# Value products of two key tiles issued as one piece, in a transformer and mixture-of-experts kernel on one NeuronCore

## The chip, the core and the metric

The kernel runs on one core of one Trainium2 chip. A core has five engines, each working through its own list of instructions in order: TensorE (PE in the profile; its weight loads are shown apart as PEld), VectorE (DVE), ScalarE (ACT), GpSimd (POOL) and SyncE (SP, which here only starts DMAs). They meet at semaphores. TensorE reads SBUF and writes PSUM, the accumulation memory, which the other engines empty.

The metric is the device time of one execution in microseconds (us), the median of several. Lower is better.

## The reference

The program is a six-layer transformer with self-attention, cross-attention and a feed-forward part, followed by one mixture-of-experts layer, over 4 batches of 512 tokens of width 256. The part that the change touches is the attention, 16 heads of width 16, run twice in each layer:

```
def _attn(q, k, v, mask):
    scores = jnp.einsum('bqhd,bkhd->bhqk', q, k) / np.float32(np.sqrt(HD))
    scores = jnp.where(mask[:, None, None, :], jnp.float32(-jnp.inf), scores)
    w = jax.nn.softmax(scores, axis=-1)
    return jnp.einsum('bhqk,bkhd->bqhd', w, v)
...
for i in range(NL):
    xn = _adaln(x, noise_emb, n1_w[i], n1_b[i])
    ... q, k, v, _rope ...
    a = _attn(q, k, v, src_mask).reshape(B, L, D) @ so_w[i].T
    x = x + a
    ... the same with the context's keys and values (cross-attention) ...
    xn = _adaln(x, noise_emb, n3_w[i], n3_b[i])
    h = jax.nn.gelu(xn @ f1_w[i].T + f1_b[i], approximate=False)
    x = x + (h @ f2_w[i].T + f2_b[i])
```

## The kernel before

**Jobs and slots.** A job is one attention of one batch: 8 in a layer (4 self, 4 cross), 48 in all. The work on a job is spread over three consecutive stretches of the program, called slots. In slot k the kernel makes the maxima of the scores of job k (pass 1), the exponentials and value products of job k-1 (pass 2), finishes job k-2 (division by the sums, output projection), and prepares queries and keys of job k+1. Slots whose finished job is a cross-attention also run the feed-forward part of that batch; they use the table of places `LONG`, the others `SHORT`. 25 short and 22 long slots have both pass 1 and pass 2 in them. The loop `Fori` runs over layers.

**Units.** A slot has 16 units (`SLOT_UNITS`). A unit is one key tile of 128 of one group of four heads: unit u is tile u % 4 of group u // 4. TensorE's order inside a unit is written out by hand: score product 0 of pass 2 (line 832), two pairs of score products of pass 1 (line 859), score product 1 of pass 2, side work of place 2u, score product 2, the value product of the previous unit (line 845), score product 3, side work of place 2u+1. Places thus run from 0 to 31, two for each unit; the tables `SHORT` and `LONG` say at which place each piece of side work stands.

**Hand-over of pass 2.** A score product of pass 2 writes one of two PSUM banks (`RING2 = 2`), ScalarE takes its exponential into `prob` (line 908), and product n may start when exponential n-2 is done. `prob` has 8 places, two units. The value product of a unit is four products of 32 columns each, which stand beside each other in the array and accumulate in `psv`; after the four tiles of a group ScalarE copies `psv` to `osum` (line 916), SP writes it to DRAM (line 525), and each of the four groups has a place of its own in `osum`.

**Hand-over of pass 1.** Two pairs of banks. VectorE takes the maximum of each pair (line 1070); pair n may start when maximum n-2 is done.

**Side work.** All of it goes through one PSUM bank, `side`, so a piece may start only when the piece before it has been read. The names: `HT` and `LT` transpose normalised rows (line 732; ScalarE reads), `HQ` and `HK` project queries and keys (line 738; VectorE reads, lines 1096 and 1097), `HV` projects values (line 746; ScalarE reads), `O` is the output projection (line 746; VectorE reads), `F1` and `F2` are the feed-forward products (lines 807 and 818; VectorE reads, lines 1106 and 1113), `M` moves the maxima. `SPLIT` are the places at which ScalarE makes the high and middle parts of queries and keys, `RECIP` and `NORM` those at which VectorE takes the reciprocal of the sums and multiplies (lines 1166 and 1170), `LN_HT` and `LN_LT` those of the normalisations, `GELU` that of the activation.

**The finish of a job.** The last group's copy stands in unit 0 of the next slot. Then SP writes it, POOL waits for the write (`pool_fence`, line 677), loads the sums (`den`), waits for the reciprocal, writes `inverse`, loads it again broadcast (shown as `nT`, line 695), VectorE multiplies at `NORM`, and TensorE does `O`. SP's order in a slot: last group's write of job k-2, context and weights where needed, first group's write of job k-1, the parts of job k+1 and the loads of its first half of heads (`load_first`, `load_second`, 12 transfers with their mask rows, lines 551, 553 and 562), the second and third group's writes, and then the loads of the second half of heads, which wait until pass 2 of the slot is over.

## Time and profile before

| | us |
|---|---|
| median of 3 runs | 4339.0 (4333.73 to 4340.74) |
| the profiled execution, device time | 4337.09 |
| its span, first to last instruction | 4335.3 |
| a short slot | 63.1 |
| long slots | 94.0 to 102.3 |
| after the last exponential (last finishes, experts) | 349.2 |

In the rows, `PE L832 MATMUL ps<-qstack,kstack ... x2` is a group of two products of source line 832. A row of a timeline gives the start in us, the time from the first start to the last end in the group, engine, line, operation, output and inputs, the shapes, the count and, in brackets, how long the engine had been idle before and who ended that. A row of a table by stretch gives the stretch, its length, and the busy time and instructions of each engine. The modelled end of a product lies behind the start of the next, so starts are compared with starts below. An f32 product is two records, one for each of its two passes.

### The profile page before, as it was taken

The numbers are of one execution on the slowest core, as the hardware profiler recorded it, in microseconds if no ns is written. First come the engines' busy times: TensorE is split into PE (matmuls) and PEld (weight loads), VectorE is DVE, ScalarE is ACT, GpSimd is POOL, SyncE is SP. The second block draws the span as 40 slices with busy tenths as digits, with TensorE's granted clock in tenths as the row PEclk, the third lists the DMA queues.
The fourth block names the chain that finished last, engine by engine and source line by source line (L and its number), as shares of the span: only waits on it lengthen the run. The fifth ranks groups of instructions, "written<-read, shape, count | busy, mean of one in ns | idle before, by whom it ended". The sixth has DMA issues, their size and how long they took to land. (4 is left out here: it accounts for less than half of the span.)

```text
span 4335.3 us, 66534 instructions
## 1 busy us (share of the span) xinstructions
PE 3833.6 (88%) x19478; PEld 1695.2 (39%) x19478; DVE 2841.1 (66%) x4476; ACT 2498.6 (58%) x4206; POOL 1148.4 (26%) x1280
## 2 busy tenths in 40 slices
PE   3899899899899899899999899999999999897558
PEld 1233344433344433344433344433344433343446
DVE  6788766688666688766688766588766688751411
ACT  1577655577655567655567655567655577654112
POOL 3233222232222232322232322232322232301043
PEclk8999999999999999999999999999999999999779
DMA  5655534445533355433356443456443366521235
GB/s 160 157 153 145 131 80 94 107 137 145 131 81 91 97 145 141 132 90 82 93 150 148 125 95 82 94 145 153 123 99 80 91 171 154 132 54 46 68 103 112
DMA packets 334220, 500.30 MB, mean 115 GB/s; under 512 B 53705, under 2 KB 242257, under 8 KB 333521
## 3 DMA queue, kind: packets, MB, share of 16 engines
q1 hardware_dynamic: 289680, 430.95, 39.0%
q0 software_dynamic: 44160, 64.73, 6.3%
q8 instruction: 184, 3.01, 0.3%
q14 instruction: 196, 1.60, 0.1%
HBM read 278.54 MB, written 222.58 MB: 116 GB/s over the span
## 5 line engine op out<-in xcount | busy, mean ns | idle before, releaser
L908 ACT ACTIVATE prob<-ps 128x512 f32<-128x512 f32 x3072 | 1751.3, 595 | 1249.8 <-PE ps L832 1246.9
L1070 DVE TENSOR_REDUCE negmax<-ps 128x2 f32<-128x1024 f32 x1536 | 1814.8, 1217 | 362.4 <-PE ps L859 332.5
L832 PE MATMUL ps<-qstack,kstack 114*128 114x512 bf16 x3072 | 1144.6, 390 | 118.0 <-ACT prob L908 99.0
L845 PE MATMUL psv<-prob,v 128*32 128x512 f32 x6144 | 826.7, 610 | 0.0
L832 PEld LDWEIGHTS ps<-qstack,kstack 114*128 114x128 bf16 x3072 | 273.9, 97 | 1269.3 <-ACT prob L908 935.7
L859 PE MATMUL ps<-kstack,qstack 49*128 49x512 bf16 x3072 | 487.8, 387 | 78.7 <-DVE negmax L1070 53.3
L677 POOL TENSOR_TENSOR pool_fence<-eps 128x1 f32<-128x1 f32 x288 | 55.2, 192 | 1688.0 <-ACT mrow L975 1026.5
L807 PE MATMUL side<-nT,wf 128*128 128x256 f32 x1536 | 375.0, 387 | 31.9 <-ACT mrow L975 18.3
L1106 DVE TENSOR_SCALAR hT<-side,f1b 128x256 f32<-128x256 f32 x384 | 167.5, 478 | 295.6 <-PE side L807 295.5
L818 PE MATMUL side<-wf,hT 128*128 128x256 f32 x1536 | 350.1, 381 | 3.5 <-DVE x L1113 1.8
L807 PEld LDWEIGHTS side<-nT,wf 128*128 128x128 f32 x1536 | 285.4, 191 | 88.2 <-ACT mrow L975 22.3
L818 PEld LDWEIGHTS side<-wf,hT 128*128 128x128 f32 x1536 | 290.2, 190 | 46.9 <-issue 4.6
L648 POOL TENSOR_TENSOR rot<-ropep 128x512 f32<-128x512 f32 x94 | 118.9, 1265 | 631.5 <-DVE ropep L1097 627.2
L651 POOL TENSOR_TENSOR rot<-rot,parts 128x1024 f32<-128x1024 f32 x94 | 200.7, 2136 | 280.7 <-ACT parts L943 280.7
L657 POOL TENSOR_TENSOR low<-rot,parts 128x1024 bf16<-128x1024 f32 x94 | 200.2, 2130 | 234.7 <-ACT parts L947 234.7
L859 PEld LDWEIGHTS ps<-kstack,qstack 49*128 49x128 bf16 x3072 | 95.2, 94 | 424.7 <-issue 309.5
L1113 DVE TENSOR_TENSOR x<-x,side 128x256 f32<-128x256 f32 x96 | 40.4, 421 | 303.5 <-PE side L818 303.5
L845 PEld LDWEIGHTS psv<-prob,v 128*32 128x32 f32 x6144 | 121.5, 108 | 274.4 <-issue 223.8
L738 PE MATMUL side<-xnT,wself 128*128 128x512 f32 x384 | 195.2, 632 | 23.6 <-DVE ropep L1097 21.0
L746 PE MATMUL side<-wcross,hT 128*128 128x256 f32 x384 | 106.0, 425 | 53.7 <-DVE hT L1170 52.6
L732 PE MATMUL side<-ident,hT 128*128 128x128 f32 x592 | 97.2, 289 | 61.6 <-DVE ropep L1097 33.7
L943 ACT ACTIVATE parts<-rot 128x1024 bf16<-128x1024 f32 x96 | 100.7, 1049 | 63.1 <-POOL rot L649 44.3
(170 smaller groups left out, 3626.8 us busy)
## 6 DMA issues: line engine op xcount, KB each, us to landing
bounce<-parts SPq DMA_DIRECT2D x480, 256.0 KB, 2.5
qstack<-bounce SPq DMA_DIRECT2D x384, 192.0 KB, 6.1
kstack<-bounce SPq DMA_DIRECT2D x384, 192.0 KB, 6.6
value_sums<-osum SPq DMA_DIRECT2D x192, 256.0 KB, 6.5
bounce<-low SPq DMA_DIRECT2D x96, 256.0 KB, 2.1
hT<-value_sums POOLq DMA_DIRECT2D x96, 256.0 KB, 4.8
nT<-inverse POOLq DMA_DIRECT2D x96, 256.0 KB, 3.8
ctxT<-in_ctxT SPq DMA_DIRECT2D x24, 512.0 KB, 5.3
```

Of the source, the lines that this page charges most:

```text
L648: nc.gpsimd.tensor_tensor(rot[:, 0, :], ropep[:, 0, :], ropep[:, 1, :], ALU.subtract).then_inc(s_rot, 1)
L651: nc.gpsimd.tensor_tensor(rot[:, :, :], rot[:, :, :], parts[w][:, 0, :, :], ALU.subtract).then_inc(s_r1, 1)
L657: nc.gpsimd.tensor_tensor(low[:, :, :], rot[:, :, :], parts[w][:, 1, :, :], ALU.subtract).then_inc(s_low, 1)
L738: mm = nc.tensor.matmul(bank, w[:, k, m * P:(m + 1) * P], act_T[:, k, :], start=(k == 0), stop=(k == KD - 1))
L807: mm = nc.tensor.matmul(bank[:, i * D:(i + 1) * D], wf1[:, kk, f * P:(f + 1) * P], nT[:, kk, th * (S // 2):(th + 1) * (S // 2)], start=(kk ...
L818: mm = nc.tensor.matmul(bank[:, 0:D], hT[th][:, f, t * P:(t + 1) * P], wf2[:, f, :], start=(f == 0), stop=(f == FT - 1))
L832: nc.tensor.matmul(ps2[:, n % RING2, :], kk[0:ROWS, h, kt * P:(kt + 1) * P], q[0:ROWS, h, :], start=True, stop=True).then_inc(s_p2full, 1)
L845: mm = nc.tensor.matmul(psv[32 * i:32 * i + 32, 0, :], v[j % 2][:, kt, (HD + 1) * h:(HD + 1) * h + 32], prob[:, 4 * (u % 2) + i, :], start ...
L859: mm = nc.tensor.matmul(ps1[:, 2 * (n % 2) + e, :], qs[j % 2][rows, 8 * e + m, t * P:(t + 1) * P], ks[j % 2][rows, 8 * e + m, :], start=Tr ...
L908: nc.scalar.activation(prob[:, 4 * (u % 2) + i, :], ps2[:, n % RING2, :], ACT.Exp, scale=HD ** -0.5).then_inc(s_prob, 1)
L1070: nc.vector.tensor_reduce(out_at, ps1[:, 2 * (n % 2):2 * (n % 2) + 2, :], AX, ALU.max, negate=True).then_inc(s_p1free, 1)
L1106: ins = nc.vector.tensor_scalar(hT[th][:, f, :], bank[:, i * D:(i + 1) * D], f1b[:, f:f + 1], None, ALU.add)
```

## The change

The order of TensorE within a unit now depends on whether u is even or odd. Value products of two units are issued as one piece, in every second unit, before score product 2 of the even unit. `prob` has ten places, for which a function gives the place of each exponential, and ScalarE takes its exponentials three and one in odd units. `osum` has two places in place of four, so a copy of groups 2 and 3 first waits for the write of groups 0 and 1, with a semaphore for each. SP issues the loads of the second half of heads at the start of the slot in which they are used, behind the last group's write, no longer at the end of the slot before. And the tables of places are new.

```diff
 SHORT = {
-    "M": [25, 0], "HV": [1, 3], "HT": [6, 8], "HQ": [9, 11], "HK": [12, 14], "O": [18, 20],
-    "SPLIT": (14, 16, 19, 21), "PARTS": 23, "RECIP": 8, "NORM": (14, 15),
+    "M": [25, 0], "HV": [1, 2], "HT": [5, 6], "HQ": [9, 10], "HK": [13, 14], "O": [18, 21],
+    "SPLIT": (13, 15, 18, 21), "PARTS": 23, "RECIP": 6, "NORM": (11, 12),
...
 LONG = {
-    "M": [27, 0], "HV": [1, 3], "HT": [6, 8], "O": [11, 12], "HQ": [14, 15], "HK": [16, 18], "LT": [17, 19],
-    "F1": [20, 21, 22, 23, 24, 25, 26, 27], "F2": [28, 29, 30, 31],
-    "SPLIT": (17, 19, 21, 23), "GELU": (24, 28), "PARTS": 25, "RECIP": 5, "NORM": (9, 10),
+    "M": [29, 0], "HV": [1, 2], "HT": [5, 6], "HQ": [9, 10], "O": [11, 13], "HK": [14, 15], "LT": [17, 18],
+    "F1": [19, 20, 21, 22, 23, 24, 25, 26], "F2": [27, 28, 30, 31],
+    "SPLIT": (13, 15, 19, 21), "GELU": (23, 27), "PARTS": 25, "RECIP": 5, "NORM": (8, 9),
...
-    "LN_LT": dict(stats=[12, 12, 12, 12], aggregate=13, guess=13, newton=14, tiles=[14, 14, 15, 15]),
+    "LN_LT": dict(stats=[13, 13, 13, 13], aggregate=14, guess=14, newton=15, tiles=[15, 15, 16, 16]),
...
-        prob = sb("prob", [P, 8, S])
+        prob = sb("prob", [P, 10, S])
-        osum = sb("osum", [P, 4, S])
+        osum = sb("osum", [P, 2, S])
...
+        def prob_at(u, i):
+            two = 2 * (u % 2) + i // 2
+            return 2 * (two - 1 if two else 3 + u // 2 % 2) + i % 2
...
 # SP, in slot()
                 if tail:
                     write_sums(k - 2, 3)
+                if k and p1:
+                    load_first(k, 1)
+                    load_second(k, 1)
...
-                if head:
-                    load_first(k + 1, 1)
-                    load_second(k + 1, 1)
...
 # PE
-            def pv(j, u):
+            def pv(j, pair):
+                if pair % 2 == 0 and (j > 0 or pair > 0):
+                    pe.wait_ge(s_os, place.jobs(j, 4) + pair // 2)
+                pe.wait_ge(s_prob, place.jobs(j, 64) + 8 * pair + 8)
+                for u in (2 * pair, 2 * pair + 1):
...
+                    if p2 and u % 2 == 1:
+                        pass2(k - 1, u, 2)
                     for what, c in plan[2 * u]:
                         side_work(k, what, c)
-                    if p2:
+                    if u and u % 2 == 0 and p2:
+                        pv(k - 1, u // 2 - 1)
+                    elif u == 0 and tail:
+                        pv(k - 2, SLOT_UNITS // 2 - 1)
+                    if p2 and u % 2 == 0:
                         pass2(k - 1, u, 2)
-                    if u and p2:
-                        pv(k - 1, u - 1)
-                    elif u == 0 and tail:
-                        pv(k - 2, SLOT_UNITS - 1)
...
 # ACT
             def copy_group(k, j, g):
-                if j > 0 and g == 0:
-                    wait_sums(act, place, j - 1)
-                act.wait_ge(s_pv, place.jobs(j, 16) + 4 * g + 4)
-                nc.scalar.activation(osum[:, g, :], psv[:, 0, :], ACT.Copy).then_inc(s_os, 1)
+                if g >= 2:
+                    act.wait_ge(s_sums[j % 2][g % 2], place.at(32 * (j // 2) + 16, 16 * NJ))
+                elif j > 0:
+                    act.wait_ge(s_sums[(j - 1) % 2][g % 2], place.at(32 * ((j - 1) // 2 + 1), 16 * NJ))
+                act.wait_ge(s_pv, place.jobs(j, 8) + 2 * g + 2)
+                nc.scalar.activation(osum[:, g % 2, :], psv[:, 0, :], ACT.Copy).then_inc(s_os, 1)
```

TensorE, a short slot from the maxima's piece of unit 12 on, before: `ps<-qstack,kstack` are score products of pass 2, `ps<-kstack,qstack` those of pass 1, `psv` the value product.

```order
L793 MATMUL side<-identb,mpart 16x128 x4
L832 MATMUL ps<-qstack,kstack 128x512
L859 MATMUL ps<-kstack,qstack 128x512 x4
L832 MATMUL ps<-qstack,kstack 128x512 x2
L845 MATMUL psv<-prob,v 32x512 x4
L832 MATMUL ps<-qstack,kstack 128x512 x2
L859 MATMUL ps<-kstack,qstack 128x512 x4
L832 MATMUL ps<-qstack,kstack 128x512 x2
L845 MATMUL psv<-prob,v 32x512 x4
```

And now, the same engine and stretch:

```order
L801 MATMUL side<-identb,mpart 16x128 x4
L840 MATMUL ps<-qstack,kstack 128x512
L867 MATMUL ps<-kstack,qstack 128x512 x4
L840 MATMUL ps<-qstack,kstack 128x512 x4
L867 MATMUL ps<-kstack,qstack 128x512 x4
L840 MATMUL ps<-qstack,kstack 128x512
L853 MATMUL psv<-prob,v 32x512 x8
L840 MATMUL ps<-qstack,kstack 128x512 x3
```

Between two pieces of value products there were four score products of pass 2; now there are eight, and four of them stand in a row between two groups of pass 1.

TensorE, units 7 and 8 of a long slot before, with the second query projection and the key projections:

```order
L738 MATMUL side<-xnT,wcross 128x512 x2
L832 MATMUL ps<-qstack,kstack 128x512
L859 MATMUL ps<-kstack,qstack 128x512 x4
L832 MATMUL ps<-qstack,kstack 128x512
L738 MATMUL side<-ctxT,wcross 128x512 x2
L832 MATMUL ps<-qstack,kstack 128x512
L845 MATMUL psv<-prob,v 32x512 x4
L832 MATMUL ps<-qstack,kstack 128x512
L732 MATMUL side<-ident,hT 128x128 x4
```

And now, units 6 and 7 of a long slot on the same engine, from the second output projection to the second key projection:

```order
L754 MATMUL side<-wcross,hT 128x256 x4
L840 MATMUL ps<-qstack,kstack 128x512
L867 MATMUL ps<-kstack,qstack 128x512 x4
L840 MATMUL ps<-qstack,kstack 128x512 x2
L746 MATMUL side<-ctxT,wcross 128x512 x2
L840 MATMUL ps<-qstack,kstack 128x512
L746 MATMUL side<-ctxT,wcross 128x512 x2
```

Two pieces of side work of one odd unit had a score product, the value product and another score product between them; now a single score product stands there.

SP, from the end of one slot into the next, before:

```order
L562 DMA qstack<-bounce 48x2048
L562 DMA kstack<-bounce 48x2048
L626 DMA expert_rows<-in_empty 16x10400
L525 DMA value_sums<-osum 128x512
L608 DMA ctxT<-in_ctxT 128x2x512
```

And now, the same engine and border:

```order
L532 DMA value_sums<-osum 128x512 x2
L634 DMA expert_rows<-in_empty 16x10400
L532 DMA value_sums<-osum 128x512
L558 DMA qstack<-bounce 48x2048
L558 DMA kstack<-bounce 48x2048
```

The write of the last group came behind the loads of the second half of heads; now these loads come behind it.

## Rows read from the trace of the kernel before

**Rows 1.** The page, busy time of each engine.

```profile
PE 3833.6 (88%) x19478; PEld 1695.2 (39%) x19478; DVE 2841.1 (66%) x4476; ACT 2498.6 (58%) x4206; POOL 1148.4 (26%) x1280
```

**Rows 2.** Stretches: a short slot; first and last first-long slot; another long slot.

```profile
1700.00:1763.13 63.13, 59.78 (x322) 19.70 (x320) 51.49 (x69) 44.82 (x80) 20.44 (x24) 1.00 0.57 146
456.37:557.24 100.87, 91.64 (x457) 44.78 (x456) 62.42 (x105) 57.12 (x91) 22.77 (x25) 0.97 0.43 112
3714.00:3813.30 99.30, 90.24 (x457) 44.14 (x454) 62.82 (x105) 56.91 (x92) 22.59 (x25) 0.98 0.41 107
1210.26:1306.26 96.00, 89.59 (x457) 44.24 (x456) 62.55 (x105) 56.68 (x90) 22.77 (x25) 1.00 0.37 90
```

**Rows 3.** Timeline, units 13 to 15 of a short slot, value products and what follows.

```profile
1756.13 0.64 PE L845 MATMUL psv<-prob,v 128*32 128x512 f32 x4
...
1756.59 0.61 PE L845 MATMUL psv<-prob,v 128*32 128x512 f32 x4
...
1757.13 0.60 PE L832 MATMUL ps<-qstack,kstack 114*128 114x512 bf16 x2
```

**Rows 4.** Timeline of the last unit of that slot, PE, ACT and DVE.

```profile
1760.01 0.61 PE L832 MATMUL ps<-qstack,kstack 114*128 114x512 bf16 x2
...
1760.44 1.08 ACT L908 ACTIVATE prob<-ps 128x512 f32<-128x512 f32 x2 [0.72 <-PE ps L832]
...
1760.55 0.60 PE L859 MATMUL ps<-kstack,qstack 49*128 49x512 bf16 x4
...
1760.93 1.18 ACT L908 ACTIVATE prob<-ps 128x512 f32<-128x512 f32 x2
...
1760.98 2.36 DVE L1070 TENSOR_REDUCE negmax<-ps 128x2 f32<-128x1024 f32 x2 [0.53 <-PE ps L859]
...
1761.09 0.39 PE L832 MATMUL ps<-qstack,kstack 114*128 114x512 bf16 x1
...
1761.58 0.39 PE L832 MATMUL ps<-qstack,kstack 114*128 114x512 bf16 x1
...
1761.90 1.07 PE L845 MATMUL psv<-prob,v 128*32 128x512 f32 x8
```

**Rows 5.** Timeline of a long slot, side work and its readers.

```profile
1342.57 0.68 DVE L1096 TENSOR_TENSOR ropep<-side,cos 128x512 f32<-128x512 f32 x1
...
1343.90 1.98 PE L738 MATMUL side<-xnT,wself 128*128 128x512 f32 x4 [0.22 <-DVE ropep L1097]
...
1352.39 0.66 PE L732 MATMUL side<-ident,hT 128*128 128x128 f32 x4 [1.60 <-DVE ropep L1097]
...
1361.32 0.38 PE L832 MATMUL ps<-qstack,kstack 114*128 114x512 bf16 x1
...
1361.52 0.88 DVE L1106 TENSOR_SCALAR hT<-side,f1b 128x256 f32<-128x256 f32 x2 [0.39 <-PE side L807]
```

**Rows 6.** Timeline of the first long slot of a layer (starts 456.37), finish of a job.

```profile
461.64 0.34 SPq L525 DMA_DIRECT2D value_sums<-osum  x1
...
470.19 0.19 POOL L677 TENSOR_TENSOR pool_fence<-eps 128x1 f32<-128x1 f32 x1 [9.66 <-DMA value_sums<-osum]
...
474.70 0.55 DVE L1166 RECIPROCAL recip<-den 128x64 f32<-128x64 f32 x1 [5.11 <-DMA den<-value_sums]
475.17 4.55 DVE L1070 TENSOR_REDUCE negmax<-ps 128x2 f32<-128x1024 f32 x4
...
476.39 0.60 PE L859 MATMUL ps<-kstack,qstack 49*128 49x512 bf16 x2 [3.59 <-DVE negmax L1070]
```

**Rows 7.** Timeline of another long slot (starts 1210.26), finish of a job.

```profile
1214.10 0.59 ACT L916 ACTIVATE osum<-psv 128x512 f32<-128x512 f32 x1
...
1231.84 0.69 DVE L1170 TENSOR_TENSOR hT<-hT,nT 128x512 f32<-128x512 f32 x1 [2.32 <-DMA nT<-inverse]
```

**Rows 8.** Waits of TensorE: us in total, times, longest.

```profile
PE side L746 <- DVE hT L1170: 52.6, 21, 15.8
```

**Rows 9.** The tile osum: from issue of its writes to landing.

```profile
DMA to landing us min/median/max: 2.0/6.5/9.4
```

More of the change, by code:

```diff
@@ L383, in layers @@
         s_os = sem("pv_group_copied")
-        s_sums = [sem(f"value_sums_written{i}") for i in range(2)]
+        s_sums = [[sem(f"value_sums_written{i}{h}") for h in range(2)] for i in range(2)]
         s_den = sem("probability_sums_loaded")
@@ L485, in wait_sums @@
         def wait_sums(eng, place, j):
-            eng.wait_ge(s_sums[j % 2], place.at(64 * (j // 2 + 1), 32 * NJ))
+            for h in range(2):
+                eng.wait_ge(s_sums[j % 2][h], place.at(32 * (j // 2 + 1), 16 * NJ))
+        def prob_at(u, i):
+            two = 2 * (u % 2) + i // 2
+            return 2 * (two - 1 if two else 3 + u // 2 % 2) + i % 2
         def norms(place, k, what, add=0):
@@ L964, in side_work @@
                     if k >= 2:
-                        act.wait_ge(s_pv, place.jobs(k - 1, 16))
+                        act.wait_ge(s_pv, place.jobs(k - 1, 8))
                     dst = v[k % 2][:, 2 * c:2 * c + 2, 0:H * (HD + 1)].rearrange("p t (h e) -> p t h e", h=H)[:, :, :, 0:HD]
```

30 lines of the change are left out of this document (15 added, 15 removed).

## The prediction

> **What bounds the kernel now.** First the page's busy times [rows 1]: TensorE is at work 88% of the span, VectorE 66%, ScalarE 58%. The question is what TensorE waits for, and that is read by slot. All short slots but those at a loop border take 63.1 us, the six long slots that come first in their layer 99.3 to 102.3, the 16 other long ones 94.0 to 99.1, 97.3 in the mean [rows 2]. Then one unit without side work, start by start [rows 4]. From the score product at 1760.01 to the one at 1762.90 a unit takes 2.88 us. Its steps: score product to the next 0.23; into and out of pass 1 0.31 each; the two pairs of pass 1 0.23 apart; score product to value product 0.31; value product to the next score product 1.00, from 1756.13 to 1757.13 [rows 3]. These add to 2.61 us; the missing 0.27 is product 2 waiting for exponential 0. So a short slot is TensorE's work, 57.6 us (16 times 2.61, and 15.8 of side work by its starts), and 5.5 us of such waits. A long one is 85.7 us of work (43.9 of it side work) and 8 to 16 us of waits.
>
> The hand-overs have fixed lengths, which I use below. Score product to its exponential 0.43 (1760.01 to 1760.44); exponentials 0.49 apart (1.08 less the 0.59 of one); exponential to the score product two later 0.65 (1760.93 to 1761.58); pass-1 pair to its maximum 0.43 (1760.55 to 1760.98); maxima 1.14 apart (2.36 less 1.22) [rows 4]; maximum to the pair two later 1.22 (475.17 to 476.39) [rows 6].
>
> **What the joint piece saves.** One pass of a value product to the next takes 0.46 us, the last pass to the score product 0.54 (1756.13, 1756.59, 1757.13) [rows 3]. Leaving costs 0.09 more than staying. Entering costs 0.31 where score product to score product costs 0.23, again 0.09. A joint piece has four passes, three of 0.46 and one of 0.54: 1.91 us. Each pair of units saves 0.18, a slot 1.45, the 48 jobs 69 us. That is all that TensorE's work loses.
>
> **What it costs in short slots.** The score products keep two banks. I follow a pair of units without side work from score product 2 of the even unit, t = 0, just behind the joint piece. Product 3 is at 0.23; exponentials 2 and 3 start at 0.43 and 0.92. Odd product 0 must wait until 0.43 + 0.65 = 1.08, exponential 0 is at 1.51. Pass 1 is at 1.39 and 1.61, product 1 at 1.92, its exponential at 2.35. Product 2 at 2.15, exponential at 2.84; product 3 at 2.35 + 0.65 = 3.00; even product 0 at 2.84 + 0.65 = 3.49. The next pass 1 would be at 3.80 and 4.02, but the second maximum of the odd unit starts at 1.39 + 0.43 + 1.14 = 2.96, so it is at 4.18. Then product 1 at 4.49, the joint piece at 4.80, and product 2 again at 6.70. Two such units take 5.76 now. So a pair without side work **loses 0.94 us**: during the 1.91 us of the joint piece ScalarE has two banks of work and VectorE two pairs, and after it eight score products run at the pace of ScalarE and of the two banks. Side work in both halves of a pair fills exactly these holes: with 1.72 us in each, the same steps give 8.50, of which 8.49 is work.
>
> A short slot by pairs of units, from the same steps with its side work and ScalarE's extra pieces in their new places, us before and after: units 0 and 1 9.47, 9.26; 2 and 3 6.57, 7.40 (ScalarE's readings of the two transposes delay the exponentials); 4 and 5 9.21, 9.06; 6 and 7 9.23, 9.06; 8 and 9 7.98, 7.79; 10 and 11 8.18, 7.9; 12 and 13 6.70, 7.13; 14 and 15 5.76, 6.70. Sum 63.1 before, 64.3 after: **1.2 us slower**, 25 slots, 30 us. The waits go from 5.5 to 8.2.
>
> **What it costs in long slots.** Work is 84.2. Waits that go: in units 8, 12 and 13 TensorE now waits 1.60 us for VectorE's queue before the transpose [rows 5] and about 2 us around the activation. Waits that come:
> - Side work in both halves of an odd unit. The second piece needs the bank read, and only one score product (0.23) lies between; before, the value product lay there too. Reading a query or key piece takes 0.25 us to start, 1.29 for two multiplications (1342.57 to 1343.90 with release) and so 1.4 us of wait; a feed-forward piece 0.3 (end at 1361.22, 0.10 before the row at 1361.32, reader at 1361.52), 0.88 and release, 1.0 us of wait [rows 5]. There are six such units: 5, 7, 9, 11, 13, 15, with 1.4, 1.4, 1.1, 1.0, 1.0 and 0.5: 6.4 us.
> - In units 5 and 7 VectorE also comes late, since two maxima (2.3 us) stand ahead of the reading, in unit 11 and 13 a little: 3.6 us.
> - VectorE stands still at the first NORM, place 8, and with it the maximum behind it. It gets there about 18.7 us into the slot. The attention rows arrive about 21.5: the last copy starts at 4.9 (3.84 before [rows 7], but the joint piece is 0.9 longer), and the chain from copy to NORM took 17.7 (1214.10 to 1231.84) [rows 7], of which the write's landing loses about 1. VectorE then loses 2.8, of which TensorE sees about 1.
> - The pair with the two transposes 1.5, as in short slots; units 8 and 9 1.5 for the second normalisation; the rest 1.1.
>
> Sum 15.1, the slot 99.3 us. For the 16 ordinary ones that is +2.0 each, 32 us.
>
> **The moved loads.** In the first long slot of a layer the sums' write is issued at 461.64, behind 12 loads, and POOL goes on only at 470.19, 8.5 us later; VectorE waits 5.11 at the reciprocal, place 5, and TensorE 3.59 for the maxima behind it [rows 6]. Behind the change nothing stands ahead of this write, and writes of osum have landed in as little as 2.0 us (median 6.5) [rows 9]. So the sums are there at about 12 us into the slot and this stop goes: 101.2 to 99.3 in six slots, 11 us. The loads themselves are hidden: issued from 5.7 to 10.8 us into the slot, needed at unit 8, past 30. What is queued behind them on SP, the context, the first group's write at unit 4 and the parts, is due later. The two places of osum cost nothing if group 1's write, issued some 4.5 us before a slot ends, lands within 9.4, the longest of all [rows 9], since the copy that needs its place starts 4.9 into the next slot.
>
> One rule speaks against this move. The Trainium skill (DMA: Bandwidth & Descriptors, Issuing engines are not separate DMA queues) says that transfers of all issuers interleave on the same 16 DMA engines. By it POOL's loads of sums and rows, which now run while SP's 12 loads are in flight, would each come later; that is rival B below.
>
> **The sum.** 30 + 32 - 11 = 51 us on the profiled execution's 4337.1: 4388. The median is 1.9 above that execution, so **4390**. Terms not in the trace: the gap between the two units inside a joint piece, bounded by 0.46 and by 0.64 (all drain paid), taken as 0.46 because the two passes of one unit also load new weights; and the contention on POOL's loads, bounded by 0 and by 3 us a long slot.
>
> **Rivals.**
> - **A, faster: O finds its rows ready.** TensorE waited 52.6 us for NORM before O [rows 8], besides the stop at the reciprocal. If the sums' write lands in 2 us and POOL's loads are not held up, the rows are there before VectorE gets to NORM, the point being 18.7 us into the slot; the hold-up of units 4 and 5 (3.4 us with what follows from it) goes, and long slots take 95.9. Price: short +30, 16 slots -22, six -32: 4315. For it: write and loads landed late while queued behind or beside the stack loads. Against it: copy later by 1.1, and two chained POOL steps.
> - **B, slower still: the moved loads hold up POOL's chain.** If rows arrive 3 us later than 21.5, TensorE loses these 3 us in each of 22 long slots: 4390 + 66 = 4456. For it: 12 loads now start 0.2 us behind the sums' write. Against it: they are over at about 17 us.
> - **C: the joint piece saves nothing**, since going from one unit's weights to the next's within it costs the same 0.18: 4390 + 69 = 4459. Rows 3 speak against it.
>
> **Chances.** My forecast 0.60, A 0.24, B 0.09, C 0.03, others 0.04. A run of this kernel can tell about 0.2%, 9 us. Faster by more than that 0.27, within 0.07, slower 0.66. The range reaches from 4290, below A, for its bound is uncertain by a microsecond per slot, to 4450, just short of B: 4290 to 4450.
>
> **What would show it.** In the profile after: short slots of 64 to 65 us, all alike; a joint piece of 1.91 us; pairs of units 14 and 15 of 6.7; in long slots TensorE waiting at the second side piece of odd units, and 98 to 101 us; no wait of 5 us at the reciprocal. Short slots at or under 63.1 would mean that a hand-over is shorter than read here; long slots under 97 that VectorE's readings come earlier than I place them.

## The result

The changed kernel takes 4702.81 us (median of 4 runs, 4699.73 to 4713.41), the kernel before 4339.87 beside it (4333.73 to 4342.37). The ratio is 1.0843, 95% interval 1.0822 to 1.0864: 363 us slower, where 51 was forecast. The profiled execution has a span of 4711.7 us.

First the page's busy times of the changed kernel, answering [rows 1]:

```profile
PE 3891.9 (83%) x19478; PEld 1806.6 (38%) x19478; DVE 2847.2 (60%) x4476; ACT 2479.0 (53%) x4206; POOL 1156.0 (25%) x1280
```

The work is the same, the engines wait longer. Then three stretches, answering [rows 2]: a short slot, a first-long one, another long one. Columns are length, busy times of PE, PEld, DVE, ACT and POOL, granted clock, DMA share and GB/s.

```profile
1847.09:1912.31 65.22, 58.98 (x321) 21.17 (x321) 50.18 (x69) 44.21 (x80) 20.89 (x24) 1.00 0.56 138
1195.10:1306.71 111.61, 92.76 (x455) 47.09 (x454) 63.31 (x105) 55.97 (x91) 22.70 (x25) 0.92 0.37 92
1306.71:1419.13 112.42, 92.82 (x458) 47.86 (x456) 64.83 (x105) 55.95 (x90) 22.70 (x25) 0.92 0.32 77
```

First-long slots grew by 11 us in the mean, the other long ones by 13, and their clock, between 0.97 and 1.00 before, is 0.92. The joint piece itself does what it should; timeline of units 14 and 15 of that short slot, answering [rows 3] and [rows 4]:

```profile
1905.68 0.39 PE L840 MATMUL ps<-qstack,kstack 114*128 114x512 bf16 x1 [0.21 <-ACT prob L922]
...
1906.86 1.92 PE L853 MATMUL psv<-prob,v 128*32 128x512 f32 x16
...
1908.72 0.60 PE L840 MATMUL ps<-qstack,kstack 114*128 114x512 bf16 x2
...
1909.88 0.39 PE L840 MATMUL ps<-qstack,kstack 114*128 114x512 bf16 x1 [0.56 <-ACT prob L922]
```

From 1906.86 to 1908.72 it takes 1.86 us (forecast 1.91), and the pair of units 6.63 (forecast 6.70, 5.76 before). This is one of the better slots: the median of that pair over the 20 short slots counted below is 7.0 us.

The finish of a job in the long slot that starts at 1306.71, answering [rows 6] and [rows 7]:

```profile
1311.51 0.60 ACT L932 ACTIVATE osum<-psv 128x512 f32<-128x512 f32 x1
...
1312.14 0.32 SPq L532 DMA_DIRECT2D value_sums<-osum  x1
1312.59 2.01 SPq L558 DMA_DIRECT2D qstack<-bounce  x1
...
1315.86 0.19 POOL L685 TENSOR_TENSOR pool_fence<-eps 128x1 f32<-128x1 f32 x1 [4.96 <-DMA value_sums<-osum]
...
1322.65 0.59 POOL L699 DMA_DIRECT2D inverse<-recip  x1 [0.28 <-issue]
1329.16 0.18 POOL L685 TENSOR_TENSOR pool_fence<-eps 128x1 f32<-128x1 f32 x1 [5.92 <-DMA inverse<-recip]
...
1334.40 0.69 DVE L1186 TENSOR_TENSOR hT<-hT,nT 128x512 f32<-128x512 f32 x1 [8.82 <-DMA nT<-inverse]
...
1336.28 0.61 PE L867 MATMUL ps<-kstack,qstack 49*128 49x512 bf16 x2 [6.28 <-DVE negmax L1086]
...
1337.65 2.81 PE L746 MATMUL side<-xnT,wself 128*128 128x512 f32 x4
```

The sums' write leaves at once, as hoped. But the write of `inverse` needs 6.5 us to be seen (1322.65 to 1329.16), NORM comes 27.7 us into the slot, VectorE stands 8.8 us, TensorE 6.3. Behind that the four products of 512 columns take 2.81 us; the same four just before the stop took 1.88: the clock is at its lower level, 1.2 GHz. The loads of the second half of heads, issued up to 1319.11, landed up to 1328.82, and `inverse` at 1328.99.

Median time from issue to landing, changed kernel and then the kernel before:

```profile
hT<-value_sums POOLq DMA_DIRECT2D x96, 256.0 KB, 9.2
...
den<-value_sums POOLq DMA_DIRECT2D x48, 32.0 KB, 5.3
inverse<-recip POOLq DMA_DIRECT2D x48, 32.0 KB, 5.5
```

Before, these three are 4.8, 2.1 and 2.4 us. Last, units 7 and 8 of the same slot, all engines:

```profile
1357.32 2.14 POOL L665 TENSOR_TENSOR low<-rot,parts 128x1024 bf16<-128x1024 f32 x1 [5.87 <-ACT parts L963]
...
1357.94 1.54 DVE L1069 SCALAR_TENSOR_TENSOR lnv<-y 128x4 f32<-128x4 f32 x1
...
1359.54 1.27 POOL L656 TENSOR_TENSOR rot<-ropep 128x512 f32<-128x512 f32 x1
...
1359.71 1.12 DVE L1071 SCALAR_TENSOR_TENSOR y<-lnv,y 128x4 f32<-128x4 f32 x1
...
1360.77 1.26 POOL L657 TENSOR_TENSOR rot<-ropep 128x512 f32<-128x512 f32 x1
1360.86 1.64 DVE L1076 TENSOR_SCALAR hT<-x,mv,y 128x256 f32<-128x256 f32 x2
...
1364.41 0.90 PE L740 MATMUL side<-ident,hT 128*128 128x128 f32 x3 [4.25 <-DVE hT L1076]
```

An operation of four columns takes 1.54 us and ends at 1359.48, when POOL's ends (1359.46). The next ends at 1360.83, POOL's at 1360.81. TensorE waits 4.25 us for the tiles behind them. And behind this stop the clock is low again, as two feed-forward pieces of the same eight products show, the first in unit 9, the other two units later:

```profile
1370.03 3.77 PE L815 MATMUL side<-nT,wf 128*128 128x256 f32 x8 [0.87 <-ACT nT L953]
...
1378.99 1.89 PE L815 MATMUL side<-nT,wf 128*128 128x256 f32 x8
```

The two stretches of this slot at the lower clock, behind NORM and behind the second normalisation (columns as above):

```profile
1332.70:1339.51 6.81, 3.23 (x7) 1.24 (x8) 5.11 (x7) 1.09 (x2) 0.00 (x0) 0.50 0.07 26
1363.42:1373.64 10.22, 8.36 (x25) 4.88 (x25) 4.35 (x6) 4.56 (x7) 2.12 (x1) 0.50 0.15 49
```

TensorE is at work for 11.6 us of them at half its speed, so the lower clock costs this slot some 5.8 us (an estimate from these two rows).

### The profile page after: what moved, and what is told of

Its sections match the earlier page's. It is cut to its first block and busy times, and to the rows that moved or that the text cites. A ratio compares the mean times of both kernels' runs of the same rounds, so it can differ in the third digit from the quotient of the medians.

```text
span 4711.7 us, 66396 instructions
## 1 busy us (share of the span) xinstructions
PE 3891.9 (83%) x19478; PEld 1806.6 (38%) x19478; DVE 2847.2 (60%) x4476; ACT 2479.0 (53%) x4206; POOL 1156.0 (25%) x1280
## 5 line engine op out<-in xcount | busy, mean ns | idle before, releaser
L922 ACT ACTIVATE prob<-ps 128x512 f32<-128x512 f32 x3072 | 1717.8, 595 | 1572.2 <-PE ps L840 1564.9
L840 PE MATMUL ps<-qstack,kstack 114*128 114x512 bf16 x3072 | 1105.0, 399 | 190.8 <-ACT prob L922 172.7
L853 PE MATMUL psv<-prob,v 128*32 128x512 f32 x6144 | 752.8, 606 | 0.0
L867 PE MATMUL ps<-kstack,qstack 49*128 49x512 bf16 x3072 | 508.5, 397 | 196.7 <-DVE negmax L1086 173.2
L815 PE MATMUL side<-nT,wf 128*128 128x256 f32 x1536 | 397.2, 404 | 47.8 <-DVE hT L1122 25.6
L853 PEld LDWEIGHTS psv<-prob,v 128*32 128x32 f32 x6144 | 171.1, 110 | 315.7 <-issue 301.5
L746 PE MATMUL side<-xnT,wself 128*128 128x512 f32 x384 | 228.9, 727 | 49.2 <-DVE ropep L1113 48.0
L1186 DVE TENSOR_TENSOR hT<-hT,nT 128x512 f32<-128x512 f32 x96 | 79.4, 829 | 239.5 <-DMA nT<-inverse 239.3
L740 PE MATMUL side<-ident,hT 128*128 128x128 f32 x592 | 112.0, 321 | 111.5 <-DVE hT L1076 109.4
L1133 DVE TENSOR_TENSOR x<-x,side 128x512 f32<-128x512 f32 x96 | 66.1, 688 | 182.9 <-PE side L754 182.9
```

The source lines that it names most:

```text
L746: mm = nc.tensor.matmul(bank, w[:, k, m * P:(m + 1) * P], act_T[:, k, :], start=(k == 0), stop=(k == KD - 1))
L815: mm = nc.tensor.matmul(bank[:, i * D:(i + 1) * D], wf1[:, kk, f * P:(f + 1) * P], nT[:, kk, th * (S // 2):(th + 1) * (S // 2)], start=(kk ...
L840: nc.tensor.matmul(ps2[:, n % RING2, :], kk[0:ROWS, h, kt * P:(kt + 1) * P], q[0:ROWS, h, :], start=True, stop=True).then_inc(s_p2full, 1)
L853: mm = nc.tensor.matmul(psv[32 * i:32 * i + 32, 0, :], v[j % 2][:, kt, (HD + 1) * h:(HD + 1) * h + 32], prob[:, prob_at(u, i), :], start=( ...
L867: mm = nc.tensor.matmul(ps1[:, 2 * (n % 2) + e, :], qs[j % 2][rows, 8 * e + m, t * P:(t + 1) * P], ks[j % 2][rows, 8 * e + m, :], start=Tr ...
L922: nc.scalar.activation(prob[:, prob_at(u, i), :], ps2[:, n % RING2, :], ACT.Exp, scale=HD ** -0.5).then_inc(s_prob, 1)
```

## The experiments

Mean length of the slots in each profiled execution, from first exponential to first exponential: 20 short slots ("short"), the 4 short ones at the loop's border, which follow long ones and in which the cross-attention's weights are loaded ("behind long"), the 6 first-long ones and the 16 other long ones; the very first slot is left out. Two of the 20, in the first and in the last layer, also load these weights. Before they took 63 us like the rest; in the changed kernel they take 73.2 and 72.2, and the other 18 take 65.7. "Median" is device time; the kernel before was at 4331 to 4337 beside these runs.

| kernel | median | short | behind long | first-long | long |
|---|---|---|---|---|---|
| before | 4339.9 | 63.1 | 69.8 | 101.1 | 97.3 |
| changed | 4702.8 | 66.4 | 72.6 | 112.3 | 110.7 |
| e1 changed, loads back | 4598.8 | 65.8 | 68.0 | 111.1 | 107.0 |
| e2 before, loads moved | 4406.7 | 63.1 | 64.5 | 103.2 | 102.1 |
| e3 joint piece, old tables, old loads | 4589.9 | 68.2 | 72.2 | 108.1 | 102.3 |
| e4 before, new tables | 4499.7 | 64.3 | 68.8 | 108.1 | 103.4 |
| e5 changed, old tables | 4690.8 | 68.6 | 68.7 | 111.2 | 109.0 |
| e6 before, loads late in long slots | 4299.7 | 63.1 | 64.4 | 100.5 | 96.3 |
| e7 changed, loads late | 4627.2 | 66.3 | 72.6 | 109.9 | 106.7 |
| e8 as e7, old long table | 4530.7 | 66.3 | 72.3 | 107.2 | 101.7 |
| e9 as e6, self weights late | 4281.9 | 63.1 | 64.5 | 95.9 | 96.7 |
| e10 as e9, reciprocal at 4 | 4244.5 | 63.1 | 64.5 | 94.8 | 95.0 |
| e11 as e6, half exponentials | 4231.6 | 60.8 | 62.2 | 100.2 | 95.9 |
| e12 as e8, half exponentials | 4447.1 | 64.2 | 69.8 | 106.3 | 99.8 |
| e13 as e6, half maxima | 4211.2 | 62.5 | 62.8 | 98.5 | 93.1 |
| e14 as e8, half maxima | 4442.1 | 65.2 | 70.9 | 104.5 | 99.6 |
| e15 as e7, half maxima | 4494.4 | 65.2 | 71.3 | 106.0 | 102.0 |
| e16 joint piece, best of all this | 4442.0 | 65.7 | 64.8 | 102.0 | 101.0 |
| e17 as e7, short POOL operations | 4516.3 | 66.1 | 72.0 | 105.4 | 102.8 |
| e18 as e6, short POOL operations | 4271.2 | 62.9 | 64.5 | 100.2 | 95.3 |

### One part at a time: e1 to e5

```diff
# e1, on the changed kernel (e2, on the kernel before: the reverse)
-                if k and p1:
-                    load_first(k, 1)
-                    load_second(k, 1)
...
+                if head:
+                    load_first(k + 1, 1)
+                    load_second(k + 1, 1)
```

> The changed kernel with one part undone: the loads of the second half of heads are issued at the end of the slot before, as in the kernel before; joint piece, places of prob and osum, and tables stay new. Theory 1 (the moved loads hold up the chain of the finish: sums written, fence, sums loaded, inverse written and loaded, NORM at 27.7 us into the slot where I had 21.5; VectorE stands there, TensorE behind it): long slots go from 109-113 to 99-102 us, NORM is at 19 to 22 us into the slot, the write of inverse lands in 2 to 3 us instead of 5.5, and the time is 4440 to 4500. Theory 2 (the new places alone put NORM too early for any chain): NORM stays past 25 us and the time is 4620 or more. Theory 3 (the joint piece starves the two banks of exponentials): also 4620 or more, with short slots at 65 to 67 in either case.

Ratio 1.0607 (1.0573 to 1.0641): 104 us less than the changed kernel, with NORM at 22 to 24 us in the 16 long slots (27 in the mean of the first-long ones), but far over 4500, and between the ranges of the theories. The mechanism of theory 1 is there; it is not the whole.

> The kernel before with one part of the change alone: the loads of the second half of heads issued at the start of the slot in which they are used, behind the write of the last group's sums. Theory 1: rows come 5 to 6 us later than before in all 22 long slots; NORM stands at place 9 here, so TensorE loses 3 to 5 us in each of 16 and the stop at the reciprocal in the six first-long slots goes: 4370 to 4440. Theories 2 and 3: no loss from these loads, and the stop at the reciprocal gone: 4300 to 4340.

Ratio 1.0176 (1.0152 to 1.0200), 75 us: theory 1. The reciprocal of first-long slots comes 12.9 us into the slot, no longer at 17 to 20, and still they take 2.1 us more, the others 4.8 more. VectorE's NORM in the long slot that starts at 1227.11:

```profile
1247.23 0.18 POOL L677 TENSOR_TENSOR pool_fence<-eps 128x1 f32<-128x1 f32 x1 [5.12 <-DMA inverse<-recip]
...
1254.60 0.69 DVE L1170 TENSOR_TENSOR hT<-hT,nT 128x512 f32<-128x512 f32 x1 [8.23 <-DMA nT<-inverse]
...
1257.16 3.69 PE L746 MATMUL side<-wcross,hT 128*128 128x256 f32 x8 [7.30 <-DVE hT L1170]
```

```diff
# e3, on the changed kernel: the edit of e1 and both old tables (e4, on the kernel before: both new tables)
-    "M": [25, 0], "HV": [1, 2], "HT": [5, 6], "HQ": [9, 10], "HK": [13, 14], "O": [18, 21],
+    "M": [25, 0], "HV": [1, 3], "HT": [6, 8], "HQ": [9, 11], "HK": [12, 14], "O": [18, 20],
...
```

> The kernel before with the joint piece, the order by parity and the new places of prob and osum, but with the old tables of places and the loads where they were. Theory 3 (the order by parity itself costs it): short slots 65 to 67 us, long slots 105 or more, 4500 or more. Theories 1 and 2: short slots 64 to 66, long slots 97 to 101, 4370 to 4420.

> The kernel before with the new tables of places alone; no joint piece, loads where they were. Theory 2 (the tables cost it: NORM at place 8, side pieces in both halves of units 5 and 7): long slots 105 or more, 4500 to 4650. Theories 1 and 3: 4330 to 4400, since without the moved loads the rows arrive at about 20 us into the slot and VectorE loses 1 to 3 us at NORM.

Ratios 1.0600 (1.0582 to 1.0617) and 1.0385 (1.0363 to 1.0407). Each theory finds its own loss: the joint piece and its places alone cost 258 us, the tables alone 168. No single cause then; and the parts don't add up (75, 258 and 168 make 501). In short slots the new table helps the joint piece (68.2 to 65.8), in long ones it hurts (102.3 to 107.0). It hurts without the joint piece too: TensorE's wait before the transposes of unit 8 is 5.0 us in the mean of e4's long slots.

```diff
# e5, on the changed kernel: both old tables, loads at the slot's start
-    "SPLIT": (13, 15, 19, 21), "GELU": (23, 27), "PARTS": 25, "RECIP": 5, "NORM": (8, 9),
+    "SPLIT": (17, 19, 21, 23), "GELU": (24, 28), "PARTS": 25, "RECIP": 5, "NORM": (9, 10),
...
```

> The changed kernel with the old tables of places: joint piece and moved loads together. If the parts add up, the moved loads cost here what they cost alone (4407 less 4332, 75 us): 4650 to 4680. If the joint piece makes VectorE late enough at NORM (place 9) that rows which come 5 us later do no harm: 4580 to 4620.

Ratio 1.0817 (1.0796 to 1.0838): 101 us for the moved loads beside the joint piece, somewhat more than alone.

### Where the loads do no harm: e6 to e8

```diff
# e6, on e2; e7, on the changed kernel
-                if k and p1:
+                if k and p1 and not is_ffn(k):
                     load_first(k, 1)
                     load_second(k, 1)
...
                 if p2:
                     write_sums(k - 1, 0)
+                if k and p1 and is_ffn(k):
+                    load_first(k, 1)
+                    load_second(k, 1)
# e8, on e7: LONG as before the change
```

> The kernel before, the loads of the second half of heads moved out of the end of the slot: in short slots behind the last group's write, in long slots behind the first group's write, some 20 us into the slot, when sums and rows have been loaded. Theory 1a (the loads cost only because they run beside POOL's chain of sums, inverse and rows): sums are there at 9 to 12 us, NORM at 19 to 21, no stop at the reciprocal in the six first-long slots: long slots 94 to 97, 4260 to 4310. Theory 1b (these 12 loads cost wherever they stand within the slot, since pass 1 of unit 8 or the transfers of unit 4 wait for them): 4380 or more, with TensorE waiting before the score product pair of unit 8.

Ratio 0.9924 (0.9908 to 0.9941): faster than the kernel before by 35 us. The loads cost only beside POOL's chain, theory 1a. Where the gain lies was not foreseen: hardly in the first-long slots (100.5), but in the four short ones behind the long (69.8 to 64.4, 22 us) and in the other long ones (97.3 to 96.3, 16 us).

> The changed kernel with the same placement of these loads: early in short slots, behind the first group's write in long ones. Theory 1a: rows at about 22 us as with the loads at the slot's end, and no late write in the first-long slots: long slots 103 to 107, 4520 to 4570. Theory 1b: no better than 4600. In either case units 5, 7 and 8 of long slots keep the waits of the new table.

Ratio 1.0668 (1.0644 to 1.0691), 76 us less than the changed kernel but over theory 1a's range; by its time alone it would fit theory 1b (4600 or more). But e6 shows that the loads do no harm at this place beside separate value products, and NORM came as theory 1a said; what is left over 4570 are other waits of the long slots. NORM at 22.8 us still stops VectorE, for less; here the slot starts at 1285.73:

```profile
1308.55 0.69 DVE L1189 TENSOR_TENSOR hT<-hT,nT 128x512 f32<-128x512 f32 x1 [4.05 <-DMA nT<-inverse]
```

> As the one before, but with the old table of places in long slots; short slots keep the new one. Joint piece and loads are thus the same, and only the places of the 22 long slots differ. Theory 2 (the new long table costs 5 us and more in units 5, 7 and 8): short slots 65, long slots 99 to 102, 4400 to 4440. Theory 3 (the joint piece cannot be fed in long slots whatever the table): long slots 104 or more, 4520 or more.

Ratio 1.0450 (1.0429 to 1.0471). The new long table costs 97 us; the joint piece with the short table the other 231. Both theories hold in part. A long slot of e8 and one of e6:

```profile
1264.01:1366.30 102.29, 90.78 (x458) 45.82 (x456) 62.92 (x105) 55.78 (x90) 22.88 (x25) 0.98 0.34 84
```

```profile
1207.99:1304.42 96.43, 89.61 (x458) 44.24 (x456) 62.56 (x105) 56.69 (x90) 22.85 (x25) 1.00 0.37 90
```

These runs split the whole by one edit at a step:

| step | us |
|---|---|
| before to e6: loads off the slot's end | -35 |
| e6 to e8: joint piece, its places, short table | +231 |
| e8 to e7: new long table | +97 |
| e7 to changed: loads beside POOL's chain | +76 |
| sum, from 4334.5 to 4702.8 | +368 |

### A faster kernel: e9 and e10

```diff
# e9, on e6
-                if k % NJ == 6 and k < NJ:
-                    sp.wait_ge(s_full, side_done)
-                    load_self(k + NJ)
...
                     write_sums(k - 1, 2)
+                if k % NJ == 6 and k < NJ:
+                    sp.wait_ge(s_full, side_done)
+                    load_self(k + NJ)
# e10, on e9, LONG
-"RECIP": 5
+"RECIP": 4
```

> The kernel with the loads late in long slots (4300 in this study), and in the first long slot of a layer the four weight loads for the next layer's self-attention moved from behind the last group's write to the end of the slot. Theory 1a (transfers that run beside POOL's chain delay the rows): NORM of these six slots, at 24.6 us now against 21.4 in the other long ones, goes to 21.4, their length from 100.7 to 96 or 97, 4260 to 4285. If these weights were not what delays it: 4295 to 4305.

> As the one before, with the reciprocal at place 4 of long slots in place of 5. The sums are there at about 9 us and the reciprocal runs at 12.7; TensorE waits 2.0 us for NORM before O. Theory 1a: inverse is written 1 to 2 us sooner, NORM and O come as much sooner, 1 to 2 us in each of 22 long slots, 20 to 40 us less than the one before. If the maxima set the time of NORM instead: no difference.

Ratios 0.9881 (0.9866 to 0.9896) and 0.9795 (0.9782 to 0.9808), as expected. First-long slots go from 100.5 to 95.9 once no weight loads run beside POOL's chain: the same mechanism as in e2, with other transfers. With the reciprocal one place earlier both kinds reach 95. Of e10, in the long slot that starts at 1186.28:

```profile
1198.92 0.58 POOL L694 DMA_DIRECT2D inverse<-recip  x1 [0.27 <-issue]
1201.01 0.18 POOL L680 TENSOR_TENSOR pool_fence<-eps 128x1 f32<-128x1 f32 x1 [1.50 <-DMA inverse<-recip]
...
1206.01 0.69 DVE L1173 TENSOR_TENSOR hT<-hT,nT 128x512 f32<-128x512 f32 x1
```

`inverse` is seen after 2.1 us where the changed kernel needed 6.5, and VectorE no longer waits at NORM. **4244.5 us beats both kernels.**

### What the joint piece waits for: e11 to e14, e16

```diff
# e11, on e6; e12, on e8 (e12's lines; e11 has 4 * (u % 2) + i as the place in prob)
-                nc.scalar.activation(prob[:, prob_at(u, i), :], ps2[:, n % RING2, :], ACT.Exp,
+                w = S if j == 0 else S // 2
+                nc.scalar.activation(prob[:, prob_at(u, i), 0:w], ps2[:, n % RING2, 0:w], ACT.Exp,
```

> The kernel with separate value products and loads late in long slots (4300 here), each exponential over 256 of its 512 columns from the second job on (half of the exponentials are left out). ScalarE then hands a bank back some 0.25 us sooner. Theory 3 (what the joint piece loses is the pace of ScalarE over two banks of scores): short slots lose most of their 5.5 us of waits, 58 to 60 us; this is the base of the next run.

> The kernel with the joint piece, new places in short slots, old ones in long slots (4531 here), with the same half exponentials. Theory 3: the joint piece now keeps its 1.45 us a short slot: short slots 1 to 1.5 us under those of the run before, where they are 2.3 us over them with whole exponentials; pair of units 14 and 15 from 6.63 to 5.3 or 5.6. If ScalarE's pace is not the cause: short slots 2 us and more over those of the run before. Long slots: under theory 3 within 2 us of the run before; if VectorE's queue sets them, still 4 to 5 us over.

Ratios 0.9766 (0.9748 to 0.9784) and 1.0264 (1.0239 to 1.0288). A short slot of the last layer, e11 and e12:

```profile
3563.16:3623.82 60.66, 58.56 (x322) 19.47 (x320) 50.72 (x69) 31.42 (x80) 20.14 (x24) 1.00 0.64 159
```

```profile
3748.77:3811.46 62.69, 58.40 (x321) 20.99 (x321) 50.60 (x69) 31.29 (x80) 20.67 (x24) 1.00 0.62 154
```

Both gain 2 us or so, and the joint piece stays 2.0 behind (2.8 in the mean of the 18 short slots without weight loads, 2.6 with whole exponentials; 3.9 in the 16 long ones); the pair of units 14 and 15 takes 6.29, not 5.3 to 5.6. Theory 3 as I had it, ScalarE's pace alone, is a miss.

But this run does not clear ScalarE. By the prediction's own steps, with each exponential 0.25 us shorter, the second maximum of the odd unit takes over and holds the pair to some 6.45 us (an estimate); the median over the short slots is 6.49. TensorE's waits in the whole program say the same: for exponentials they are 206.4 us in e8 and 121.7 in e12, for maxima 46.7 and 83.1.

```diff
# e13, on e6; e14, on e8; e15, on e7
-ps1[:, 2 * (n % 2):2 * (n % 2) + 2, :], AX, ALU.max
+ps1[:, 2 * (n % 2):2 * (n % 2) + 2, 0:S // 2], AX, ALU.max
...
-                                     scale=HD ** -0.5).then_inc(s_prob, 1)
+                                     scale=HD ** -0.5 / 64).then_inc(s_prob, 1)
```

> The kernel with separate value products and loads late in long slots (4300 here), each maximum over 256 of the 512 columns of its two banks (half of the scores are left out of the maximum, and the exponentials are scaled down so that they stay finite). A maximum of 1.22 us becomes some 0.68, which frees some 17 us of VectorE in a slot. Base of the next two: if VectorE's queue is what its long slots wait for, 97 goes to 90 to 93.

> The kernel with the joint piece, new places in short slots and old ones in long slots (4531 here; long slots 102.3, 5.2 over those with separate value products), with the same half maxima. Theory V (the joint piece loses by VectorE's queue: its readings of the side bank come later behind the maxima): long slots within 1 us of the run before, short ones 1 us under it. Theory S (what is lost is the wait of the second side piece of an odd unit for the reading of the first, and the hand-over of the two score banks, whose lengths a short maximum does not change): long slots still 4 to 5 us over the run before, short ones 1 to 2 over it.

Ratios 0.9725 (0.9706 to 0.9745) and 1.0258 (1.0238 to 1.0279), 231 us apart as e6 and e8 are. Long slots are 93.1 and 99.6: with 16 us less for VectorE the joint piece loses 6.5, not less than the 5.4 before. In the 18 short slots without weight loads it loses 2.2 in place of 2.6. Theory V falls; theory S is the nearer one, though both its ranges (4 to 5, 1 to 2) are passed. What stays in e14 are waits as this one in unit 7, where between two side pieces stands one score product:

```profile
1277.65 1.98 PE L749 MATMUL side<-xnT,wself 128*128 128x512 f32 x4
1279.47 0.38 PE L843 MATMUL ps<-qstack,kstack 114*128 114x512 bf16 x1
1281.11 1.98 PE L749 MATMUL side<-xnT,wself 128*128 128x512 f32 x4 [1.26 <-DVE ropep L1116]
...
1292.71 3.19 PE L749 MATMUL side<-xnT,wself 128*128 128x512 f32 x4
```

The last line, unit 9 of the same slot, has the same four products at the lower clock, though no stop over 2 us came before.

The larger part are waits for the score banks. TensorE's waits for exponentials in e6, e8 and e14 (us in total, times, longest):

```profile
PE ps L835 <- ACT prob L911: 97.4, 215, 1.7
...
PE ps L843 <- ACT prob L925: 206.4, 447, 1.5
...
PE ps L843 <- ACT prob L925: 228.2, 494, 1.8
```

With half maxima they rise, as those for maxima rose with half exponentials. Each of the two hand-overs seems to cover the other, and no run shortens both at once. By the same steps as above half maxima alone leave the pair of units 14 and 15 at 6.55 (median measured 6.77), both together would leave 5.8, against 5.24 for separate pieces in e11.

```diff
# e16, on e8: the edit of e9, and
-"RECIP": 5
+"RECIP": 4
...
-"NORM": (11, 12)
+"NORM": (14, 15)
```

> The joint piece with all that the runs so far found better: loads late in long slots, self-attention weights at the end of the slot, old places in long slots with the reciprocal at 4, and in short slots NORM at 14 and 15 in place of 11 and 12 (rows arrive 31.7 us into the short slot that follows the long ones, where VectorE stands 4 us and the slot takes 72 us). Expected: that slot 66 us, first-long slots 101 to 102, other long slots 100 to 101, 4430 to 4460. The same set with separate value products is at 4245, so that the joint piece itself costs 190 to 210 us here; 4350 or less would mean that its loss was one of placement.

Ratio 1.0268 (1.0244 to 1.0291), in the middle of the range; the slots behind the long ones go from 72.3 to 64.8 with NORM back at place 14. With all else equal or better placed the joint piece is 197 us behind e10.

### What the new long table waits for: e15, e17, e18

> As the one before, with the new table of places in long slots (4627 here, long slots 106 to 109, 4.3 us over the old table). The new table's extra waits stand before the second key projection (2.6 us) and the transposes of unit 8 (3.2 to 4.4 us), both behind VectorE. Theory V: they shrink to under 1.5 us each, and the long slots are within 1.5 us of the run before. Theory S: still 4 us over it.

Ratio 1.0379 (1.0358 to 1.0400), 52 us over e14 where the whole maxima had 97. The wait before the second key projection goes from 2.6 to 1.5 us, that before the transposes of unit 8 only to 3.9. VectorE's queue explains the first, not the second.

```diff
# e17, on e7; e18, on e6
-                nc.gpsimd.tensor_tensor(rot[:, 0, :], ropep[:, 0, :], ropep[:, 1, :], ALU.subtract).then_inc(s_rot, 1)
+                W = 64
+                nc.gpsimd.tensor_tensor(rot[:, 0, 0:W], ropep[:, 0, 0:W], ropep[:, 1, 0:W], ALU.subtract).then_inc(s_rot, 1)
...
```

> The kernel with the joint piece, both new tables and loads late in long slots (4627 here), POOL's four operations on each query and key (rotation and low part) over 64 of their 512 columns; the rest of these columns is left as it is, so queries and keys are not the true ones. Theory P: in the changed kernel POOL works on the query just when VectorE makes the factors of the second normalisation, and VectorE's small operations end when POOL's end: 1.54 us for one of 128x4 that takes 0.15 elsewhere, 1.12 for another, 1.31 for a row tile of 0.41; they hold the transposes of unit 8 up. With POOL's operations short they go back to 0.15, 0.16 and 0.41, the 4.4 us wait before these transposes to about 1.7, and long slots lose 2.5 to 3 us: 4560 to 4575. Theory N (the wait is the length of the chain from O over statistics and factors to the tiles): durations fall, but the wait stays over 3.5 and the time over 4600.

> The same for the kernel with separate value products and the old tables (4300 here), as the base of the run before: there POOL's operations fall on VectorE's only in one pair of row tiles (1.75 us in place of 0.74) and in NORM (1.37 in place of 0.68 in a quarter of them). Theory P: 0 to 1 us a long slot, 4275 to 4300. If short operations on POOL save time by another way (parts written sooner, fewer bytes), this run loses as much as the one before, 55 us or more.

Ratios 1.0408 (1.0382 to 1.0434) and 0.9844 (0.9823 to 0.9866). e17 gains 111 us, e18 only 29, so 82 us are special to the joint piece with the new long table: theory P, with more than I gave it. That it is the table shows in the first and third operation of the factors: 42 of 144 took over 0.4 us in e4 (new tables, no joint piece), none in e8 (joint piece, old long table) and none before. Of e17, the long slot that starts at 1259.27:

```profile
1306.59 0.15 DVE L1073 SCALAR_TENSOR_TENSOR lnv<-y 128x4 f32<-128x4 f32 x1
...
1306.97 0.29 DVE L1075 SCALAR_TENSOR_TENSOR y<-lnv,y 128x4 f32<-128x4 f32 x1
1307.29 0.73 DVE L1080 TENSOR_SCALAR hT<-x,mv,y 128x256 f32<-128x256 f32 x2
...
1309.93 0.65 PE L744 MATMUL side<-ident,hT 128*128 128x128 f32 x4 [1.12 <-DVE hT L1080]
```

The 1.54 us are 0.15 again, and the wait before the transposes falls to 1.1. Nor does the clock fall behind it in this slot's units 8 and 9 (the feed-forward piece takes 1.99 us, not 3.77), which fits a gain larger than the wait. The 29 us of e18, a little more than forecast, are what short POOL operations bring without it.

## Why the prediction was wrong

The direction stood, and so did most of the waits that the likeliest case named; the moved loads cost where a gain was forecast, and the size was off. By kinds of slot: the 16 long ones brought 214 us where 32 stood in the sum, the six first-long ones 67 where a gain of 11 stood, and the short ones 78 where 30 stood. By the forecast's own steps:

- **Joint piece 1.91 us**: 1.86. Right; rival C falls.
- **Short slots, +1.2.** The slot at 1847.09 has by pairs 8.99, 7.70, 9.38, 9.59, 7.88, 7.62, 7.43 and 6.63 us, each within 0.55 of the forecast, and 65.2 in all, 0.9 over it. That is a good slot: the mean of the 18 without weight loads is 65.7, since some have units at the lower clock or longer waits (unit 0 of the slot at 1779.62 takes 6.92 us, that of the next 5.39; the median of the first pair is 9.83 where 9.26 was forecast). So +2.6 in place of +1.2, 47 us in the 18.
- **The six short slots with weight loads** were taken as short ones like the others. Rows arrive there at about 33 us, as the cross-attention's weights load beside them, and NORM had moved from place 14 to 11, so VectorE stands 6 us: 9.9 and 9.2 us more in the first and last layer, 2.8 in the four at the loop's border, which took 69.8 us already, and 7.5 on the kernel with late loads (72.3 against 64.8, e16).
- **"The loads themselves are hidden"**, with the rows at 21.5 us: the step that failed first. They are hidden from their own readers, not from POOL's chain: NORM at 25 to 29 us, 76 us (e7). I had read that they are over by about 17 us, where the last of them landed 22.1 us into the slot shown, and that the chain's transfers of 32 KB would land as before; they took 5.3 and 5.5 us in place of 2.1 and 2.4. **Rival B**, with 0.09, was this mechanism, and its 66 us came near the price, in part by luck, since its 3 us a slot stood on no row. The row that bore on it was there: in [rows 6] a write behind 12 loads took 8.5 us. The rule of the Trainium skill that the prediction cites (DMA: Bandwidth & Descriptors, Issuing engines are not separate DMA queues) agrees with e2 and e7, 75 and 76 us.
- **First-long slots, 11 us gained** by the stop at the reciprocal. The stop went, in e2 too, and the rows were late all the same. Both the loads and the self-attention's weights stood in their way (e9).
- **NORM costs TensorE about 1 us.** It was 6.3 in the slot shown and 5.2 in the mean of the 16, and the sum had no term for what follows a stop: products at the lower clock, some 1.5 us more in unit 5.
- **Second side pieces and late VectorE, 10.0 us**: the six waits of the slot at 1306.71 are 1.33, 2.60, 1.25, 0.94, 1.49 and 0.46, 8.1 in all. Right in kind and size. That half maxima take none of the long slots' loss away (e13, e14) speaks for hand-overs, not queue.
- **"Units 8 and 9 1.5 for the second normalisation"**: 8.1 us, the other large miss: some 4.4 of them are the stop and 3.7 products at the lower clock behind it, for which the sum had no term either. I costed the order of VectorE's operations and not what POOL does meanwhile: with HQ ahead of O in the table, POOL's work on the query falls on the factors and tiles (e17, 82 us).

So this long slot has 28 us over its work where 15.1 stood in the sum: some 7 more at NORM and 6.6 more in units 8 and 9, and of the 28 some 5.8 are no waits but products at the lower clock. **Rival A** fell with its condition.

**Left open.** Of the 231 us of joint piece and short table some 50 are the six short slots with weight loads, where NORM stands too early. In the rest the waits of second side pieces and between score products are seen, and neither a shorter exponential nor a shorter maximum alone removes them. That the hand-overs with two banks of scores and one of side work set them is argued, not shown: the run with both shortened is missing, and a third bank of scores was not tried, since it would have to be taken from pass 1 or from the side work.

How much of the loss is the lower clock is only bounded. One less the granted clock, times the span, is 147 us before (0.966 of 4335.3) and 330 in the changed kernel (0.930 of 4711.7). So at most some 180 of the 363 us are the clock, and less, as TensorE stood still in part of those stretches. By steps it is at most 70 of the 231 (e6 0.969, e8 0.955), 88 of the 97 (e7 0.937) and 38 of the 76.

## What to carry to other kernels

A transfer that is early enough for its own reader can still be in the way of a short chained one: before moving loads, list which chains of small transfers (write, wait, load) run in the stretch they move to, and move them behind that chain. Joining pieces saves their seams but widens the distance between the other pieces; with few banks on the other hand-overs that costs more than the seam (0.18 us saved a pair; 0.9 lost net in the slot shown, 1.2 in the median). And when a table of places moves an operation of VectorE, look at what GpSimd does at that place.

## What the hardware showed that I had not expected

- **VectorE's operations are held until GpSimd's ends.** In the changed kernel 14 of the first factor's operations (128x4) met a large one of POOL and took 1.54 us in the median, the other 58 took 0.16; 21 of the tiles' (128x256, SBUF only) took 1.32, the other 267 took 0.41. Not held in the same trace: 317 maxima that read PSUM (1.22 either way), 81 additions of the feed-forward bias from PSUM (0.47), 84 statistics from SBUF (0.41). The Trainium skill (SBUF — State Buffer, Who interferes with whom) says that VectorE and GpSimd share a pair of ports, and that an operation of VectorE with two inputs in SBUF, or in a mode that uses both ports, blocks until GpSimd's ends where that one, reading SBUF, was issued first; these rows agree with it.
- **How long a transfer of 32 KB takes depends on what else is under way**: `inverse` is seen after 2.1 us in e10's slot shown, where the 12 loads come later, and after 6.5 us in the changed kernel's, 0.2 us behind the landing of the last of these loads.
- **The clock can fall without a long stop**: long slots of e8 and e14 have 0.98, and in e14 unit 9 has products at half speed (3.19 us against 1.98) behind waits of under 2 us.
